# A deformable and a depthwise convolution in one stream of chunks: VectorE's evacuation between two of its copies, stacked taps, merged biases, two more chunks of lag

## What is computed

```python
def reference(x, ...):
    x = x + _L0_conv_ref(_gn(x), w_off, b_off, w_dcn, b_dcn)
    x = x + _L1_conv_ref(_gn(x), w1, b1, w2, b2)
    return x

def _L0_conv_ref(x, w_off, b_off, w_dcn, b_dcn):
    off = (sigmoid(conv2d(x, w_off, b_off)) - 0.5) * 2.0      # two offsets per channel and pixel
    ...
    sampled = v00*(1-wy)*(1-wx) + v01*(1-wy)*wx + v10*wy*(1-wx) + v11*wy*wx
    return conv2d(sampled, w_dcn, b_dcn)

def _L1_conv_ref(x, w1, b1, w2, b2):
    pooled = x.mean(axis=(2, 3))
    kernels = (relu(pooled @ w1 + b1) @ w2 + b2).reshape(b, 32, 3, 3)
    return depthwise_conv(x, kernels)                         # another 3x3 kernel per image and channel
```

## Time and profile before

| | |
|---|---|
| median of 3 runs | 1694.75 us (1694.44 to 1696.19) |
| the profiled execution: its own time | 1700.7 us |
| its span, first to last instruction | 1698.9 us |
| TensorE busy | 1574.7 us, 93% |
| VectorE busy | 1356.8 us, 80% |
| ScalarE busy | 1052.9 us, 62% |
| GpSimd busy | 313.5 us, 18% |
| mean granted TensorE clock | 0.967 of full speed |

### The profile page before, as it was taken

One profiled execution on the slowest core, in us unless ns is written; L12 is line 12 of the kernel. 1 busy time (PEld: TensorE's weight loads), 2 busy tenths in 40 slices (PEclk: granted clock), 3 DMA queues, 4 the chain that ended last, 5 costly groups with the idle time before them and its releaser, 6 DMA issues.

```text
span 1698.9 us, 30216 instructions
## 1 busy us (share of the span) xinstructions
PE 1574.7 (93%) x12176; PEld 671.1 (40%) x12176; DVE 1356.8 (80%) x1264; ACT 1052.9 (62%) x1586; POOL 313.5 (18%) x381
## 2 busy tenths in 40 slices
PE   3779878999999999999999999999999999999887
PEld 1333334333443334433443334433444334533343
DVE  3899989798879978799887987798787898889700
ACT  4766556765777566666667656676575765655413
POOL 3000312012230221203230122301403031300010
PEclk9899999999999999999999999999999999999979
DMA  7355446666666665666666666666565765556436
GB/s 231 107 178 169 140 124 198 174 200 202 191 210 196 173 205 169 193 203 195 184 207 184 199 198 179 194 197 191 168 213 171 220 171 164 177 158 193 132 89 199
DMA packets 225195, 307.73 MB, mean 181 GB/s; under 512 B 16656, under 2 KB 167552, under 8 KB 224992
## 3 DMA queue, kind: packets, MB, share of 16 engines
q1 hardware_dynamic: 223632, 304.42, 60.5%
q0 software_dynamic: 1424, 1.38, 0.3%
HBM read 190.11 MB, written 38.14 MB: 134 GB/s over the span
## 4 chain that ended last, share of the span: by engine, by line
PE 54%; DVE 19%; ACT 11%; issue 6%; DMA 5%; POOL 3%; SPq 2%; DVEq 0%; ACTq 0%; POOLq 0%
PE z L357 25%; PE dc L397 13%; PE dw L427 9%; DMA st<-in_planes 4%; DVE nb L718 3%; DVE nb L713 3%; DVE nb L716 3%; PE sm L483 2%; ACT dv L540 2%; PE dc L427 2%; DVE xv L706 2%; DVE nb L720 2%; DVE nb L722 2%; ACT mv L547 2%; DVE nb L707 2%
## 5 line engine op out<-in xcount | busy, mean ns | idle before, releaser
L357 PE MATMUL z<-xv,wos 128*64 128x384 f32 x4608 | 775.5, 493 | 33.9 <-issue 22.6
L357 PEld LDWEIGHTS z<-xv,wos 128*64 128x64 f32 x4608 | 333.6, 137 | 454.0 <-issue 445.8
L397 PE MATMUL dc<-sr,wds 128*32 128x384 f32 x2304 | 453.4, 525 | 25.7 <-DVE yr L739 25.6
L397 PE MATMUL dc<-sh,wds 128*32 128x384 f32 x2112 | 411.8, 527 | 0.0
L699 DVE COPY_PREDICATED nb<-mu,xv 128x2280 f32<-128x2280 uint16 x96 | 268.8, 2800 | 100.0 <-ACT mu L547 99.1
L427 PE MATMUL dw<-yr,wy 128*64 128x388 f32 x672 | 258.1, 506 | 4.6 <-ACT ot L575 3.7
L427 PE MATMUL dw<-yh,wy 128*64 128x388 f32 x672 | 258.2, 506 | 0.0
L540 ACT ACTIVATE du<-z,ob 128x768 f32<-128x768 f32 x96 | 86.3, 899 | 275.2 <-PE z L357 275.2
L397 PEld LDWEIGHTS dc<-sr,wds 128*32 128x32 f32 x2304 | 123.4, 111 | 296.4 <-issue 294.8
L561 ACT ACTIVATE nb<-xv 128x2292 f32<-128x2292 f32 x96 | 202.7, 2112 | 41.7 <-issue 41.3
L706 DVE COPY_PREDICATED xv<-mv,xv 128x768 f32<-128x768 uint16 x96 | 102.5, 1067 | 90.6 <-ACT mv L547 67.7
(11 more groups left out here) (118 smaller groups left out, 1619.4 us busy)
## 6 DMA issues: line engine op xcount, KB each, us to landing
xv<-in_x SPq DMA_DIRECT2D x272, 384.0 KB, 4.7
yr<-in_xr SPq DMA_DIRECT2D x96, 392.0 KB, 7.7
out<-ot SPq DMA_DIRECT2D x96, 388.0 KB, 3.7
yh<-yr SPq DMA_DIRECT2D x179, 196.0 KB, 6.8
st<-in_planes SPq DMA_DIRECT2D x56, 576.0 KB, 7.1
sh<-sr SPq DMA_DIRECT2D x160, 194.0 KB, 2.8
sh<-sr SPq DMA_DIRECT2D x32, 145.5 KB, 2.5
yr<-in_planes SPq DMA_DIRECT2D x8, 576.0 KB, 12.0
```

Source lines behind the costliest of these rows:

```text
L357: last = nc.tensor.matmul(acc[m], weights[:, kx, :], view[:, :, kx:kx + W], start=kx == 0, stop=kx == 2)
L397: last = nc.tensor.matmul(dc[m, q, 0:NB * PAIRS], weights[:, kx, q], view[:, :, cols], start=first, stop=final)
```

## The change

1. VectorE: `evacuate` no longer follows `sample`. Inside `sample(i)`, between the large copy and the two small ones, stands `evacuate(i - 4)`. The four last chunks are evacuated in a loop tail. `y_square(i - 4)` on ScalarE stays where it was.
2. Taps: the weights `w2` of the two channel halves are stacked on 128 partitions, `hid` has two columns, and `taps` is 8 matmuls of two columns in place of 16 of one. `hidden` moves from the start to the end of TensorE's step 4, `taps` to step 5, `y_bias` to step 7.
3. The two groups of biases share one turn of the small PSUM bank (`ob` and `db` become one).
4. `DW_STEP` goes from 17 to 19, the ring `YS` from 15 to 17 slots; `ypad` has two buffers; `set_y_edges` stands one step later.
5. GpSimd sets the padding of the next image's first chunks before `set_last_edge` and before `pivot`, which waits for a DMA.

```diff
-XS, SS, YS, HS = 3, 3, 15, 4
+XS, SS, YS, HS = 3, 3, 17, 4
-DW_STEP = 17
+DW_STEP = 19
...
@@ tensor @@
             def x_biases(b):
                 pe.wait_ge(wo_ok, b + 1)
-                biases("ob", b, C_OB, (wos[b % 2][:, 0], wos[b % 2][:, 1]), nmx[b % 2][:])
                 pe.wait_ge(wd_ok, b + 1)
-                small_turn("db", b)
+                small_turn("ob", b)
...
             def taps(b):
                 small_turn("tap", b)
-                for t in range(TAPS):
-                    last = nc.tensor.matmul(sm[:, C_TAP + t:C_TAP + t + 1], w2r[:, t, :], hid[:],
+                for t in range(TAPS // 2):
+                    last = nc.tensor.matmul(sm[:, C_TAP + t:C_TAP + TAPS:TAPS // 2], w2r[:, t, :], hid[:],
                                             start=True, stop=True)
...
@@ tensor, the loop @@
-                if 0 < b <= B and o == 4:
-                    hidden(b - 1)
-                if 0 < b <= B and o == 5:
+                if 0 < b <= B and o == 7:
                     y_bias(b - 1)
...
-                if 0 < b <= B and o == 4:
+                if 0 < b <= B and o == 5:
                     taps(b - 1)
...
                 if 0 < b <= B and o == 3:
                     y_means(b - 1)
+                if 0 < b <= B and o == 4:
+                    hidden(b - 1)
@@ vector @@
                 nc.vector.copy_predicated(q[:, :, :, 1:W - 1], m3[:, :, :, 1:W - 1],
                                           v[:, :, :, 3:W + 1]).then_inc(lerp, 1)
+                if 0 <= n - DCN_STEP - 1:
+                    evacuate(n - DCN_STEP - 1)
                 m1 = mv[s][:].bitcast(U16)
...
                 if i < TOTAL:
                     sample(i)
-                if 0 <= i - DCN_STEP < TOTAL:
-                    evacuate(i - DCN_STEP)
+                if TOTAL <= i <= TOTAL + DCN_STEP:
+                    evacuate(i - DCN_STEP - 1)
@@ gpsimd, the loop @@
+                if b < B and o == 0:
+                    if b == 0:
+                        set_pads(i + 1)
+                    set_pads(i + 2)
                 if 0 < b <= B and o == 0:
                     set_last_edge(b - 1)
                 if b < B and o == 0:
-                    if b + 1 < B:
-                        pivot(b + 1)
-                    set_pads(i + 1)
-                    set_pads(i + 2)
                     set_first_edge(b)
                 if b < B and o < SS:
                     set_s_pads(i)
...
+                if b + 1 < B and o == 0:
+                    pivot(b + 1)
...
                 if b + 1 < B and o == 11:
+                    set_pads(i + 1)
                     x_weights(b + 1)
-                    set_pads(i + 1)
+                    set_pads(i + 2)
```

More of the change, by code:

```diff
@@ L98, in small_order @@
 def small_order():
-    order = [("xm", 0), ("xv", 0), ("ob", 0), ("db", 0)]
+    order = [("xm", 0), ("xv", 0), ("ob", 0)]
     for b in range(B + 1):
@@ L104, in small_order @@
         if b + 1 < B:
-            order += [("xm", b + 1), ("xv", b + 1), ("ob", b + 1), ("db", b + 1)]
+            order += [("xm", b + 1), ("xv", b + 1), ("ob", b + 1)]
     return {key: i for i, key in enumerate(order)}
@@ L130, in block_kernel @@
         yf = sb("yf", [P, 2, Q, PW])
-        ypad = sb("ypad", [P, Q, PW])
+        ypad = [sb(f"ypad{s}", [P, Q, PW]) for s in range(2)]
         ot = [sb(f"ot{s}", [P, NB, Q, OW]) for s in range(2)]
@@ L437, in average @@
                     .then_inc(small, 1)
[L439 to L446, removed]
             def x_mean(b):
@@ L457, in x_biases @@
                 pe.wait_ge(wo_ok, b + 1)
-                biases("ob", b, C_OB, (wos[b % 2][:, 0], wos[b % 2][:, 1]), nmx[b % 2][:])
                 pe.wait_ge(wd_ok, b + 1)
-                small_turn("db", b)
+                small_turn("ob", b)
+                mean = nmx[b % 2][:]
+                for i in range(2):
+                    for kx in range(3):
+                        for m in halves:
+                            nc.tensor.matmul(sm[m, C_OB + i:C_OB + i + 1], wos[b % 2][:, i, kx], mean,
+                                             start=kx == 0, stop=kx == 2)
                 for q in range(Q):
@@ L464, in x_biases @@
                             last = nc.tensor.matmul(sm[C * g:C * g + C, C_DB + q:C_DB + q + 1], wds[b % 2][:, kx, q],
-                                                    nmx[b % 2][:], start=kx == 0, stop=kx == 2)
+                                                    mean, start=kx == 0, stop=kx == 2)
                 last.then_inc(small, 1)
@@ L475, in hidden @@
                 for q in range(Q):
-                    last = nc.tensor.matmul(sm[0:HID, C_HID:C_HID + 1], w1r[:, q], pooled[:, q:q + 1],
+                    last = nc.tensor.matmul(sm[:, C_HID:C_HID + 1], w1r[:, q], pooled[:, q:q + 1],
                                             start=q == 0, stop=q == Q - 1)
@@ L619, in read, with hidden_read @@
                 nc.scalar.activation(dst, src, func, **kw).then_inc(small_rd, 1)
+            def hidden_read(b):
+                act.wait_ge(small, SMALL["hid", b] + 1)
+                for half_of, m in enumerate((slice(0, HID), slice(HID, P))):
+                    last = nc.scalar.activation(hid[m, half_of:half_of + 1], sm[m, C_HID:C_HID + 1], ACT.Relu,
+                                                bias=b1c[m], scale=1.0 / (2 * G))
+                last.then_inc(small_rd, 1)
             def off_bias(b):
@@ L625, in off_bias @@
                 nc.scalar.activation(ob[b % 2][:, 1:2], sm[:, C_OB + 1:C_OB + 2], ACT.Identity,
-                                     bias=bo[:, 1:2], scale=0.5).then_inc(small_rd, 1)
+                                     bias=bo[:, 1:2], scale=0.5)
+                for q in range(Q):
+                    last = nc.scalar.activation(db[b % 2][:, q:q + 1], sm[:, C_DB + q:C_DB + q + 1], ACT.Identity,
+                                                bias=bd[:, q:q + 1])
+                last.then_inc(small_rd, 1)
                 act.wait_ge(small_rd, SMALL["ob", b] + 1)
[L628 to L631, removed]
             act.wait_ge(piv, 1)
@@ L658, in _ @@
                 if 0 < b <= B and o == 5:
+                    hidden_read(b - 1)
+                if 0 < b <= B and o == 6:
                     read("tap", b - 1, tapr[:], sm[:, C_TAP:C_TAP + TAPS])
@@ L677, in _ @@
                     size(i, 1)
-                if 0 < b <= B and o == 4:
-                    read("hid", b - 1, hid[:], sm[0:HID, C_HID:C_HID + 1], ACT.Relu, bias=b1c[:], scale=1.0 / (2 * G))
-                if 0 < b <= B and o == 5:
+                if 0 < b <= B and o == 7:
+                    wait(act, o_done, Q * CHUNKS * (b - 1))
                     read("wb", b - 1, wb[:], sm[:, C_WB:C_WB + Q], bias=mvy[:, 0:1])
@@ L938, in _ @@
                     set_y_pads(b - 1)
-                if 0 < b <= B and o == 5:
+                if b >= 2 and o == 5:
+                    set_y_edges(b - 2)
+                if 0 < b <= B and o == 6:
                     y_weights(b - 1)
```

37 lines of the change are left out of this document (18 added, 19 removed).

## The result

| | median | runs | ratio to before, 95% interval |
|---|---|---|---|
| before | 1694.6 us | 4 | |
| changed | 1982.7 us | 4 (1977.2 to 1986.4) | 1.170 (1.167 to 1.174) |

What follows compares the result with a forecast made beforehand. It took a VectorE-ScalarE loop of 15.00 us, beside TensorE's 15.12, as the bound, growing to 17.70. Loop +245.7, boundaries -99 and ends +3 gave +150 us on 1694.75, so 1845 us, range 1815 to 1885.

Steps and rivals of the forecast that it cites:

- The loop evacuation, square, `mv`, small copies, 17.70 us: VectorE and ScalarE wait on each other; the large copy enters their loop, taking it from 15.00 to 17.70 us.
- The 245.7 us: Stream's added time: 91 steps at 2.70 us more each, from the large copy entering the loop.
- 0.76 + 5.84 + 5.95 + 2.70 = 15.25 us: TensorE's loop from evacuation over deformable and depthwise work, offsets and large copy back to evacuation; under 17.70 us.
- the cover for boundary work: TensorE's idle time in every step, about 2.5 us, said to hide extra work at image boundaries.
- The third rival: TensorE falls to its lower clock and bounds again: loop 3.45 us longer, 18.7 us, about 1935 us; 7%.
- The boundary term, -99 us: Time lost beyond the loop, nearly all at image boundaries, shrinks from 125.8 to 27 us.
- The padding: TensorE's offsets waiting for GpSimd's padding at image boundaries, 22.6 us in all, removed by the new place of `set_pads`.
- The ends: Before and after the stream: two more depthwise chunks and a later evacuation, less halved taps and hidden GpSimd work; +3 us.
- The faster rival: Evacuation fills VectorE's 0.77 us idle before the small copies and adds nothing; about 1640 us; 3%.
- A reading that does not hold: Kernel before: the square waited 0.74 us at the head of ScalarE although `z` for `dv` was there.
- The signs of being wrong: Copies under 17.4 us apart, TensorE's stream clock below 0.9, or boundary steps over 4 us beyond neighbours.

Runs made afterwards that it cites:

- e4: Changed kernel with ScalarE's `finish(c, 0)`, and the read of `wb` it needs, moved ahead of the square: 1844.8 us, ratio 1.089.
- e8: Kernel before with only the new order of GpSimd's padding: 1673.8 us, ratio 0.988.
- e6: Changed kernel with 2 more matmuls of 384 columns per step, results unused, while TensorE waits for the depthwise bank: 1913.1 us, one run.
- e3: Changed kernel with ScalarE's square (and an image's totals) moved behind `finish(c, 0)`: 1654.9 us, ratio 0.978.

## Why the prediction was wrong

- **The loop evacuation, square, `mv`, small copies, 17.70 us: right.** The large copies 5 to 11, ahead of the first depthwise chunk, where the bank plays no part, are 17.62 to 17.70 us apart, and so are most in e4. The 245.7 us for it stand.
- **The step that failed** is the one that says of TensorE's loop "0.76 + 5.84 + 5.95 + 2.70 = 15.25 us" and "TensorE idles about 2.5 us in every step and this is the cover for boundary work". The 5.84 us took the second depthwise half as if it could follow the first deformable half at once. It needs the bank `dw`, and `finish`, which empties it, stands behind the square on ScalarE too. In place of 0.76 + 2.19 us up to the second depthwise half it is 5.87 us, so that TensorE's loop is 18.22 us at full clock. TensorE does idle about as long as forecast or longer (213.1 / 83 = 2.6 us for the bank), but inside the loop that sets the step, where it covers nothing. The prediction followed what waits behind the square up to `mv` and stopped there; the instructions behind `mv` in the same queue were also late, and one of them had another engine waiting.
- **The clock.** The third rival had TensorE as the bound at its lower clock, 1935 us, with 7%. It had the right engine, and the half-speed stretch added 1.6 us rather than 3.45. The prediction set it aside because "afterwards it will be busy 15.12 of 17.70 us, the same share" as in steps with a clock of 0.96. From 440 to 1660 us the share is as forecast, 1038.2 of 1220 us or 85%, and the clock of 0.94 is near. What the share could not tell is the cost. From the fifth to the 11th copy the changed kernel's clock is 0.87, lower still, and its steps are 17.65 us: there VectorE's loop is the longer one and the slow matmuls are covered. Where TensorE's loop sets the step, each fall costs 1.6 us. In e4 about 20 of the 75 steps hold a fall, and its loop of 17.66 us is not lengthened; why there are fewer (the clock from 440 to 1660 us is 0.97) was not tested.
- **The boundary term, -99 us, failed with the cover.** The 125.8 us were to shrink to 27 because TensorE had 2.45 us to spare. In the changed kernel it has none. In e4, where it has them, the stream takes 1738.9 - 95.4 = 1643.5 us (its first number is the fifth copy's start) against 1637.7 forecast. This leaves 32.8 us beyond 91 x 17.70, for 27 forecast. The padding, which needs no cover, was forecast at 22.6 us and measured 21 as a net sum (e8). The ends, forecast at +3 us, are 288.1 - 285.0 = +3.
- **How the 138 us divide.** From the changed kernel to e6 (clock held up) 70 us, from e6 to e4 (bank released early) 68. The second is 0.55 us in some 75 ordinary steps, 41 us, and about 27 that boundary work costs without the cover. This last part is a remainder and was not measured alone; most of it lies in the steps that begin with the large copies of steps 11, 0 and 3 of an image (20.1, 19.8 and 20.4 us in e6, 18.3, 18.2 and 18.6 in e4). e6 is a single run.
- **The faster rival** (1640 us, 3%) needed the evacuation not to hold ScalarE. e3 makes that so, and gives 1654.9; but even then the evacuation is better left at the end of the step, by 38 us.
- **A reading that does not hold.** The prediction says that the square held up ScalarE in the kernel before "although the `z` for `dv` was there". In that step TensorE is at the offsets until 765.60, so at 764.30 the second half of `z` was not finished. The changed kernel shows what was meant: the square waits until 585.44, the offsets end at 583.5, and the tanh into `dv` still starts only at 587.11, behind square and abs.
- **The signs of being wrong did not fire.** Copies under 17.4 us apart, a clock below 0.9 and a boundary step over 4 us beyond its neighbours were named. Behind the 21st copy none of these occurs (ahead of it the clock was 0.89), and the stream is 138 us too long. No upper bound for the distance of the copies was among them.

## What to carry to other kernels

When an instruction that waits is given a later release, list everything behind it in its engine's order, not only the next value on the path, and for each the engine and buffer that it frees; single-buffered PSUM banks are the first to look for. The list of waits alone does not show how near such a release is to its limit. In e3 the same row looks much like that of the kernel before:

```profile
PEld dw L427 <- ACT ot L571: 39.5, 56, 1.4
```

but in the step at 1330 us `finish` ends there at 1330.26, 0.67 us ahead of the weight load at 1330.93, and in the kernel before 0.13 us ahead of it. So take the distance from the releasing instruction's end to the start of what it releases: what is left there is all that a move may use up, and here, with the evacuation 2.70 us later, TensorE's wait for the bank became 2.6 us. And where an engine's idle time is counted as cover, ask whether it lies inside the loop that sets the step; there it covers nothing, and a fall of TensorE's clock that was free elsewhere is paid in full.

## What the runs showed of the hardware

TensorE's granted clock fell to its lower level behind an idle stretch of 2.82 us in the middle of a busy step: not at once, but after 0.71 us of matmuls at full speed, and then for 3.31 us, in which half of the depthwise and half of the deformable matmuls ran (0.85 us each in place of 0.49 and 0.51). The length of the idle stretch did not decide alone. In the same kernel, stretches of 2.83 us (until 590.12) and of 3.33 us (until 948.05) were followed by no fall, and one of 0.97 us (until 570.34), behind 1.95 us of taps with two columns each, was. The runs leave open what decides.

Two added matmuls of 384 columns in each such stretch, with a wait of 102.5 us still left in total, took the stream's mean clock from 0.94 to 1.00 and 70 us off the kernel (one run); four took off 59 us (four runs). Extra work made the kernel faster. The Trainium skill ("TensorE: Matmul & The Clock Gate", on HAM oscillation) describes a matmul engine that waits in every turn of a loop and starts the next turn at the lower level. This trace agrees in part: the fall comes in about 50 of 75 steps, 1.6 us each, and in the step shown it sets in 0.71 us behind the end of the wait.
